# Interleaving two heads' score matmuls with two PSUM bank fills in a fused attention and conditional-convolution kernel

## What is computed

```
x = x + proj(attention(group_norm(x)))      # 4 heads of 64 channels over 1024 pixels, softmax over keys
rw = sigmoid(mean_pixels(x) @ router.T + b) # 8 gates for each image
W1, W2, W3 = sum_e rw[e] * expert_e         # 1x1 (256->64), 3x3 (64->64), 1x1 (64->256)
x = relu(x + bn3(conv3(relu(bn2(conv2(relu(bn1(conv1(x)))))))))
```

## Time and profile before

| | |
|---|---|
| median of three runs | 2053.33 us (2052.08 to 2059.14) |
| the profiled execution's own time | 2058.66 us |
| its span in the trace | 2056.9 us |
| TensorE busy | 1891.7 us, 92% |
| GpSimd busy | 1453.5 us, 71% |
| ScalarE, VectorE busy | 1089.9 us (53%), 1042.4 us (51%) |
| mean granted TensorE clock | 0.989 of full speed |
| chain that ended last | TensorE 78%, issue 7%, VectorE 6%, ScalarE 5% |

### The profile page before, as it was taken

The page is one execution under the profiler, slowest core; times in us unless marked ns, Lnnn a source line. Parts: engine busy times, 40 slices in busy tenths (PEclk is TensorE's granted clock), DMA queues, the critical chain, the costliest instruction groups (busy, mean ns, idle before and its releaser), DMA issues.

```text
span 2056.9 us, 28956 instructions
## 1 busy us (share of the span) xinstructions
PE 1891.7 (92%) x8388; PEld 1073.6 (52%) x8388; DVE 1042.4 (51%) x1812; ACT 1089.9 (53%) x1498; POOL 1453.5 (71%) x829
## 2 busy tenths in 40 slices
PE   4999999999999999999999999999999999999986
PEld 4555555555555555555555555555555555555542
DVE  5546455454544546455364554545455364554514
ACT  3545546555465555646455465564655546455452
POOL 3667768677686776857767587776868758677582
PEclk9999999999999999999999999999999999999998
DMA  3112322223232222322223222232322223222132
GB/s 90 46 49 62 108 83 73 82 62 92 86 88 76 59 86 82 97 77 74 80 61 107 77 77 82 62 92 87 87 82 56 83 82 97 77 68 70 57 103 82
DMA packets 94113, 161.58 MB, mean 79 GB/s; under 512 B 25600, under 2 KB 26368, under 8 KB 94080
## 3 DMA queue, kind: packets, MB, share of 16 engines
q1 hardware_dynamic: 94080, 161.17, 26.9%
HBM read 101.61 MB, written 17.04 MB: 58 GB/s over the span
## 4 chain that ended last, share of the span: by engine, by line
PE 78%; issue 7%; DVE 6%; ACT 5%; POOL 2%; DMA 1%; DVEq 0%; ACTq 0%; SPq 0%; POOLq 0%
PE PV L722 22%; PE SB L582 13%; PE MS L688 10%; PE S L706 9%; PE S L709 8%; PE SB L626 5%; PE SB L662 4%; DVE K L959 2%; POOL psum_p L556 2%; PE SB L671 1%; PE SB L649 1%; PE MS L616 1%; DVE mx L922 1%; ACT Q L810 1%; ACT hpad L840 1%
## 5 line engine op out<-in xcount | busy, mean ns | idle before, releaser
L556 POOL TENSOR_TENSOR psum_p<-psum_p,prob 128x1024 f32<-128x1024 f32 x384 | 914.2, 2381 | 197.5 <-ACT prob L795 178.6
L922 DVE TENSOR_REDUCE mx<-MS 128x1 f32<-128x512 f32 x998 | 641.8, 685 | 597.3 <-PE MS L688 589.3
L795 ACT ACTIVATE prob<-S 128x1024 f32<-128x1024 f32 x512 | 519.5, 1023 | 301.3 <-PE S L709 297.8
L722 PE MATMUL PV<-prob,V 128*64 128x512 f32 x2048 | 475.6, 607 | 0.0
L706 PE MATMUL S<-Q,K 128*128 128x512 f32 x1024 | 445.0, 435 | 13.0 <-ACT prob L795 10.0
L709 PE MATMUL S<-Q,K 128*128 128x512 f32 x1024 | 402.1, 393 | 0.0
L688 PE MATMUL MS<-K,Q 128*128 128x512 f32 x998 | 336.8, 405 | 34.1 <-ACT zrow L828 11.9
L722 PEld LDWEIGHTS PV<-prob,V 128*64 128x64 f32 x2048 | 137.4, 138 | 259.9 <-issue 229.7
L706 PEld LDWEIGHTS S<-Q,K 128*128 128x128 f32 x1024 | 192.5, 188 | 152.4 <-issue 86.8
L688 PEld LDWEIGHTS MS<-K,Q 128*128 128x128 f32 x998 | 184.8, 187 | 123.4 <-DVE mx L922 52.2
L513 POOL TENSOR_TENSOR mix<-mix,ex 128x768 f32<-128x768 f32 x90 | 165.0, 1833 | 74.7 <-ACT ex L856 72.8
(11 more groups left out here) (153 smaller groups left out, 1804.8 us busy)
## 6 DMA issues: line engine op xcount, KB each, us to landing
ex<-in_experts_dram SPq DMA_DIRECT2D x122, 384.0 KB, 3.5
xin<-in_x_dram SPq DMA_DIRECT2D x64, 256.0 KB, 3.0
K<-K SPq DMA_DIRECT2D x128, 128.0 KB, 2.3
Q<-Q SPq DMA_DIRECT2D x128, 128.0 KB, 2.2
x<-in_x_dram SPq DMA_DIRECT2D x64, 256.0 KB, 3.5
out_dram<-y SPq DMA_DIRECT2D x64, 256.0 KB, 2.1
rz<-z_dram SPq DMA_DIRECT2D x126, 128.0 KB, 2.9
V<-v_next SPq DMA_DIRECT2D x16, 512.0 KB, 2.9
```

The costliest lines, as they stand in the source:

```text
L556: nc.gpsimd.tensor_tensor(acc, first_in, prob[:, s % PBUF, :, :], ALU.add).then_inc(add_done, 1)
L722: last = nc.tensor.matmul(PV[own(a), :], V[:, b // NH, kt, a * D:a * D + D], prob[:, s % PBUF, a, :], start=(kt == 0), stop=(kt == KT - 1))
L795: nc.scalar.activation(prob[:, s % PBUF, :, :], S[:, s % 2, :, :], ACT.Exp, scale=D ** -0.5).then_inc(exp_done, 1)
L922: nc.vector.reduce_max(mx[:, b % 2, nh, m:m + 1], MS[:, nh, :], AX.X).then_inc(max_read, 1)
```

## The change

In each place the four score matmuls came first and the two fills behind them. Now the first head's two score matmuls come first, then the fill of bank 0, then the second head's two, then the fill of bank 1. The wait on `exp_done` stays ahead of the first head; `s_done` is still raised by the last matmul of the second head; the waits on lent banks, and those on the new pair's Q and K, stand ahead of the fill of bank 0 as before. The tables of all engines are unchanged, and so is everything on the other engines.

```diff
-            def max_fill(i, b, m, lent):
+            def max_fill(i, b, m, lent, parts=range(NH)):
...
-                if m == 0:
+                if m == 0 and parts[0] == 0:
...
-                for nh in range(NH):
+                for nh in parts:
...
-            def scores(i, s):
+            def scores(i, s, heads=range(2)):
...
-                wait(pe, exp_done, STEPS * i + s - 1)
-                for a in range(2):
+                if heads[0] == 0:
+                    wait(pe, exp_done, STEPS * i + s - 1)
+                for a in heads:
...
-                last.then_inc(s_done, 1)
+                if heads[-1] == 1:
+                    last.then_inc(s_done, 1)
...
                 for n in range(STEPS):
-                    if n + 2 < STEPS:
-                        scores(i, n + 2)
-                    elif not last:
-                        scores(i + 1, n + 2 - STEPS)
                     at = fill_at(i, n, last)
+                    for a in range(2):
+                        if n + 2 < STEPS:
+                            scores(i, n + 2, (a,))
+                        elif not last:
+                            scores(i + 1, n + 2 - STEPS, (a,))
+                        if at:
+                            max_fill(*at, lent, (a,))
+                            lent = []
                     if at:
-                        max_fill(*at, lent)
-                        lent = []
                         fills = 2 * (32 * at[0] + 8 * at[1] + at[2] + 1)
```

## The result

The changed kernel takes 2074.03 us (median of four runs, 2072.87 to 2077.66) against 2053.66 us for the kernel before: a ratio of 1.0097, 95% interval 1.0075 to 1.012. It is slower, by 20 us where 17 were forecast. The profiled executions lie closer together, 2071.3 us of span against 2056.9, as the profiled run of before was 5 us above its median. Of these 14.4 us, 16.3 arise between the start of the second image and that of the last; the first image and the end give 1.9 back.

The account below looks back on a forecast made before the run. TensorE's queue was taken as the bound; the place terms summed to +1.02 us an image, +14.6 us in all, plus 2 us for clock falls: 2053.3 + 16.6 = 2070 us, range 2054 to 2084.

Parts of the forecast that it names:

- Held first fills: First fill waits with two score matmuls now behind it: place 28 +0.46, place 0 +0.46, places 12 and 24 +0.28 each.
- Rival B: No change: `zrow` in time in places 12 and 24, ScalarE's slack hides place 19; +0.01 us an image, 2053; chance 0.15.
- Gains (places 7, 13 to 15): Place 7: second fill no longer held, -0.28 us; places 13 to 15: earlier reductions release a job, net -0.37 us.
- rival A: Blocked places are free, their matmuls only replacing later waits; gains alone, 0.91 us an image, 2040 us; chance 0.10.
- Places 18 and 19: Place 18's held fill makes exp 0.70 us later; ScalarE delays place 19's eviction of `v`: +0.45 us an image.
- One or two falls more: Place 19: added idle brings one or two more clock falls of 1.53 us each; +2 us in all.
- rival C: The clock never falls, as short idle times between fills go: 14.6 - 9.2 = +5.4, 2059 us; chance 0.10.
- rival D: The clock falls in every image as place 19 gets longer: +28.4, 2082 us; chance 0.10.
- Place 28's score matmul behind the held fill: Sign: in places 28 and 0 a score matmul follows the first fill, and the place is 0.46 longer.
- 42 waits on the reductions under 50 us: Sign: fewer waits on VectorE's reductions (L922) than 115, and under 50 us.
- 125.3 us an image: Sign: an image takes about 125.3 us where the clock holds, against 124.3; wrong if 124.3 or less.
- the count of waits on `zrow`: Sign: fills of places 12 and 24 show a wait on `zrow`, its count going from 13 to over 40.

Follow-up runs that it names:

- bank-wise waits: Changed kernel, but each lent bank's wait stands only ahead of that bank's fill: 2056.54 us in one run, beside a kernel before of 2057.78.
- gains without losses: Changed kernel with old order in places 0, 1, 12, 18, 24 and each lent bank's wait ahead of its fill: 2044.71 us against 2058.22 before, ratio 0.9938.
- fill first: Changed kernel with the first fill ahead of both heads' scores, the second behind them: 2112.34 us in one run, +54.6 over its kernel before.

## Why the prediction was right

**The bound and the method.** TensorE's queue bounds the kernel, the change only reorders it, and the sum of the waits' changes in one steady image gave the result. Image for image it holds to 0.05 us: +1.02 forecast, +1.0 measured. The closeness of the totals, +16.6 forecast against +20.4 by the medians and +14.4 by the profiled executions, says less: the terms were off both ways (place 19 too high, the gains too large), and a fall of the clock more or less moves a total by 1.5 us. The forecast's reading of the earlier trace rows, up to 4% of the span in waits of TensorE, took weight loads for matmuls; ahead of the matmuls it was 34.1 us, under 2%. No term of the sum was taken from it.

**Held first fills (places 28, 0, 12, 24).** Right in all four, in size too. That the wait for `zrow` bites in places 12 and 24, where the trace of before showed no wait at all, was read from a handshake in another place: the earlier trace rows gave 0.14 us from ScalarE's end to the fill, the trace after gives 1213.90 to 1214.03, 0.13:

```profile
1213.52 0.38 ACT L832 ACTIVATE zrow<-MS 128x256 f32<-128x256 f32 x1 [2.10 <-PE MS L616]
1213.64 0.40 PE L710 MATMUL S<-Q,K 128*128 128x512 f32 x1
1214.03 0.19 PEld L688 LDWEIGHTS MS<-K,Q 128*128 128x128 f32 x1 [0.43 <-issue]
1214.03 0.49 PE L688 MATMUL MS<-K,Q 128*128 128x512 f32 x1
1214.36 0.40 PE L707 MATMUL S<-Q,K 128*128 128x512 f32 x1
```

Rival B, which had this wait free and place 19 hidden, is out.

**Gains (places 7, 13 to 15).** Right in kind, a little smaller than forecast: -0.26 for -0.28 and -0.30 for -0.37. With place 1's -0.25 they make 0.8 us against 1.8 us of losses, and rival A, by which only they would count, is refuted by the kernel with the new order in the five held places alone.

**Places 18 and 19.** The mechanism was right, the size high: +0.34 for +0.45. The eviction of `v` came 0.33 us later in all (2.61 - 2.38, and place 18's 0.10), where I had 0.48 from ScalarE's queue; exp itself was late by the forecast 0.7 us, but an eviction queued behind exp starts 0.11 us before exp's recorded end (1236.66 against 1235.76 + 1.01), so the slack ahead of it had been 0.33, not the 0.22 of the bracket in the earlier trace rows.

**The clock.** Granted clock and duration of place 19 in two images, after, beside the earlier trace rows:

```profile
1108.78:1121.24 12.46, 10.65 (x59) 5.04 (x57) 2.76 (x7) 5.15 (x11) 11.30 (x7) 1.00 0.45 136
1234.05:1248.11 14.06, 12.14 (x59) 5.66 (x58) 2.76 (x7) 5.15 (x11) 12.44 (x8) 0.88 0.41 122
```

Eight images look like the second, six did before, and a fall costs 1.4 to 1.6 us in both kernels. "One or two falls more" fits this trace, but its cause is not shown, so this part of the forecast may be luck. The other kernels had, in place 19, three (new order in the held places), four (old order there; bank-wise waits), five (gains without losses; fill first, which had five elsewhere too), six and six (old order in place 18, in place 13). That does not follow the length of place 19: at the same 12.47 us there were eight in the changed kernel, three with the new order in the held places, and four with bank-wise waits. The clock fell more often than before, not never, which takes rival C out, and in eight images of 15, not in all, which takes rival D out. The rule weighed there, of the Trainium skill's "TensorE: Matmul & The Clock Gate", section "A second HAM failure mode: psum-queue depth-cycling", is not tested by it: it would need smoother fills, and the matmuls of the fills stood idle longer here, 52.4 us against 34.1.

**What I said would show it.** Place 28's score matmul behind the held fill, place 7's earlier P·V, 42 waits on the reductions under 50 us, and 125.3 us an image all came. The sign of the 42 waits was weaker than it seemed, as it came from the weight loads; the matmuls' waits on the reductions grew. One sign did not come as written: the count of waits on `zrow` went from 13 to 20, not over 40. In place 12 the fill is held by 0.16 us (it starts 0.39 us behind its neighbour), but the matmul ahead of it is recorded until 1214.04, so its own row has no bracket. The row of its weight load has one, 0.43 us, put down to "issue". Weight loads of the fills of places 12 and 24 have such a bracket 31 times in this trace and never in the one of before, 5 of them under `zrow` and 26 under "issue". So the waits are there, under another name.

## What to carry to other kernels

In an in-order queue a wait is as dear as the work standing behind it that could have run ahead of it. Before moving an instruction with a wait, list the places where it is held by an event that does not move with it, count what the move puts behind it there, and weigh that against the stalls that the move cures elsewhere. Where one table serves all places, the answer may differ by place, and a wait that guards two buffers belongs ahead of the use of each, not of the first.

## What was not expected of the hardware

A matmul that is held for less than the overlap of recorded matmuls has no idle time in its own row: a start 0.39 us after its neighbour's, where 0.23 is usual here, is a stall of 0.16 us. Starts against starts show it, and so does the idle time of its weight load, whose releaser may be given as "issue". A list that adds up matmuls and weight loads of one line can fall while TensorE waits longer, as 115 waits to 42 did here beside 34.1 us to 52.4.

The length of a steady place repeats to 0.05 us or less in the kernels before and after, so that one profile separates effects of 0.1 us that the times of whole runs, which spread by 3 to 8 us, could never show. Place 19 behind an old-order place 18 is the exception, with 0.2 us between images and once 0.85. What spreads the whole runs is at least in part the number of images in which the clock fell, at 1.4 to 1.6 us each.
